# Weight loads issued ahead of the wait for h and p in the gated recurrence of a single-core kernel

## The chip, the cores and the metric

The kernel runs on one core of a Trainium2 chip. The time is the device time of one execution in microseconds; the median of three runs is compared. TensorE (PE) works on a pair of instructions: a weight load (PEld in the profile) puts a 128x128 matrix into the array, and a product (MATMUL) streams the moving operand through it. VectorE (DVE), ScalarE (ACT), GpSimd (POOL) and SyncE (SP, which issues transfers) have queues of their own; semaphores order them.

## The reference, cut to what matters

A mixture of experts (up, gelu, down, four experts and a shared one) is added to x, then a gated recurrence over 1024 time steps runs over the result, for a batch of 2 and 256 features:

```python
def step(h, xs):
    xzt, xrt, xht = xs
    z = jax.nn.sigmoid(xzt + h @ U_z + vz)
    r = jax.nn.sigmoid(xrt + h @ U_r + vr)
    hh = jnp.tanh(xht + r * h @ U + vh)
    h_new = (1.0 - z) * h + z * hh
    return (h_new, h_new)
_, out_t = jax.lax.scan(step, h0, xs)
x = x + jnp.swapaxes(out_t, 0, 1)
```

## The kernel before

The time steps are cut into 16 chunks of 64. Before the loop stands a start of some 55 us (transposes of x, the experts' work on the first chunk, the split of the recurrent matrices). Then a loop over 1024 steps runs the recurrence, and the experts' work on the next chunk is dealt out in small pieces, `side(c, t, window)`, into the two pauses that TensorE has in each step; the order of TensorE's work is written out by hand in that loop.

The recurrent matrices are held as two halves of 16 bits, `u_high` and `u_mid`, and h and p (r times h) likewise as a high and a low part. So each gate takes 12 products a step in `recur`: 8 of the high part (2 output halves x 2 input halves x 2 matrix halves, `HIGH_PRODUCTS`) and 4 of the low part (`LOW_PRODUCTS`). Each product has a weight load of its own, 128x128. One step on TensorE is:

- wait for h_high, 8 products for r; wait for h_low, 4 products for r; the last one signals ScalarE (`preact`);
- 12 products for z, with no wait;
- side work of window 0 (one piece: an `up` or a `down` product of the experts, fp32, which runs as two passes);
- wait for p_high, 8 products for c (the candidate); wait for p_low, 4 products for c; signal;
- side work of window 1 (two pieces). Then the next step.

ScalarE makes tanh of r, z and c as they come (`gate_tanh`, line 395), and one gelu of the side work in some steps (line 389). VectorE makes p_cur from tanh of r and h (line 610), p_low (line 613), the two blend coefficients (lines 618 and 620), then the new h with a scan instruction (line 626), h_low (line 629), half of h (line 630) and the step's output (line 635). The semaphore `part_ready` counts p_high, p_low, h_high and h_low, four a step; TensorE waits on it four times a step. In the last chunk there is no further expert work, and `idle` products of 256 or 384 columns (line 649) stand in the two pauses.

A wait written as `pe.wait_ge` is carried by the instruction that follows it on TensorE. A matrix product written as `mm` becomes a load and a product, and the load, which comes first, carries the wait.

Of the kernel before, what the change touches and what calls it, by code (L numbers as in the profile page):

```python
# [15 lines left out]
P = 128  # L16
GATES = 3
R, Z, C = range(GATES)
# [19 lines left out]
def moe_gru_kernel(nc, x, cond, gate_w, gate_b, time_w, time_b, ew1, eb1, ew2, eb2, sw1, sb1, sw2, sb2,  # L38
                   w_z, u_z, c_z, b_z, w_r, u_r, c_r, b_r, w_h, u_h, c_h, b_h, branch_mask, out):
    B, T, D = x.shape  # L40
    E, _, H = ew1.shape
    BR = E + 1
    KC = D // P
# [81 lines left out]
    with ctx:  # L125
# [3 lines left out]
        def pb(name):  # L129
            return ctx.enter_context(nc.psum_tensor(name, [P, RANK], F32))  # L130
# [67 lines left out]
        gate_ps = [pb("r_ps"), pb("z_ps"), pb("c_ps")]  # L198
# [446 lines left out]
        def _(pe):  # L645
            mm = pe.matmul

            def idle(columns, bank=0, start=False):
                mm(up_ps[bank][:, IDLE_AT:IDLE_AT + columns], ident16[:, :], keep_warm[:, 0:columns],  # L649
                   start=start, stop=True, skip_group_check=True)  # L650
# [3 lines left out]
            for i in range(XT):  # L654
# [4 lines left out]
                for k in range(KC):  # L659
                    for b in range(B):  # L660
                        at = (k * B + b) * P
# [29 lines left out]
            def up(c, i, k):  # L691
                e, j = TILES[c][i]
                n = TILE0[c] + i
                if k == 0:
                    if c <= 1 and j == 0:
                        pe.wait_ge(up_in[e], 16)
                    if n >= 2:
                        pe.wait_ge(gelu_done, n - 1)
                last = mm(up_ps[n % 2][:, 0:COLS], up_w[:, e, k, j * P:(j + 1) * P],  # L699
                          feat[:, k, c * COLS:(c + 1) * COLS], start=(k == 0), stop=(k == KC - 1),  # L700
                          skip_group_check=True)
                if k == KC - 1:
                    last.then_inc(up_done, 1)

            def down(c, i, m):
                e, j = TILES[c][i]
                n = TILE0[c] + i
                if m == 0:
                    if c <= 1 and j == 0:
                        pe.wait_ge(down_in[e], 16)  # L710
                    if e == E:
                        pe.wait_ge(gelu_done, n + 1)
                    elif c == 0:
                        pe.wait_ge(scaled_first, SCALED[n])
                    else:
                        pe.wait_ge(scaled, SCALED[n])
                last = mm(y_ps[:, m * COLS:(m + 1) * COLS], down_w[:, e, j, m * P:(m + 1) * P],  # L717
                          hidden[:, n % TILES_HELD, :], start=False, stop=(m == KC - 1), skip_group_check=True)
                if m == KC - 1:
                    last.then_inc(down_done, 1)  # L720

            def output_bias(c, m):
                if m == 0:
                    if c > 0:
                        pe.wait_ge(feat_ready, c * KC)
                    if c <= 1:
                        pe.wait_ge(rows_made, c + 1)
                mm(y_ps[:, m * COLS:(m + 1) * COLS], bias2_rows[:, m * P:(m + 1) * P],  # L728
                   branch_rows[:, c * COLS:(c + 1) * COLS], start=(m == 0), stop=False, skip_group_check=True)

            def project(c, g, m, k):
                at = (c % 2) * REGION + m * COLS
                mm(gate_ps[g][:, at:at + COLS], wx[:, g, k, m * P:(m + 1) * P], feat[:, k, c * COLS:(c + 1) * COLS],  # L733
                   start=False, stop=False, skip_group_check=True)

            def turn_body(n):
                pe.wait_ge(body_added, n + 1)
                for k in range(KC):
                    last = pe.transpose(rows_ps[:, k * P:(k + 1) * P], out_feat[:, n % 2, k, :], ident[:, :])  # L739
                last.then_inc(turned, 1)  # L740

            first_tiles = len(TILES[0])
            for i in range(first_tiles + FIRST_LAG):
# [4 lines left out]
                if i == 4:  # L748
                    pe.wait_ge(agg_made, 1)
                    for q in range(3):  # L750
                        for k in range(KC):
                            mm(y_ps[0:B, 64 + 2 * E:64 + 3 * E], agg[:, q, k, :], gate_w_sb[:, q, k, :], start=False,
                               stop=False, skip_group_check=True)
                    mm(y_ps[0:B, 64 + 2 * E:64 + 3 * E], ones[0:1, 0:B], bias_row[:, 2 * E:3 * E], start=False,
                       stop=True, skip_group_check=True).then_inc(logits_made, 1)
# [36 lines left out]
            HIGH_PRODUCTS = [(m, k, w) for m in range(KC) for k in range(KC) for w in (u_high, u_mid)]  # L792
            LOW_PRODUCTS = [(m, k, u_high) for m in range(KC) for k in range(KC)]

            def recur(s, g, low, product, last_of_sum=False):
                m, k, w = product
                c, t = divmod(s, CT)
                at = (c % 2) * REGION + m * COLS + t * B

                width = B if last_of_sum else min(FILL if g == C else H_FILL, RANK - at)  # L800
                if g == C:
                    moving = p_low[:, k, 0:width] if low else p_bits[:, k, 1:2 * width:2]
                elif low:
                    moving = h_low[:, 0:width // B, k * B:(k + 1) * B]
                else:
                    moving = h_bits[:, 0:width // B, 4 * k * B + 3:4 * (k + 1) * B:4]
                return mm(gate_ps[g][:, at:at + width], w[:, g, k, m * P:(m + 1) * P], moving, start=False,  # L807
                          stop=last_of_sum, skip_group_check=True)

            def side(c, t, window):  # L810
                for what, *of in SIDE[t, window]:
                    if what == TURN:
                        n = c * BODIES + t // STEPS
                        if n > 0:

                            pe.wait_ge(blended, (c * CT + t + 1) * BLEND_STEP + 2)
                            if n > 1:
                                pe.wait_ge(turned_copied, n - 1)
                            turn_body(n - 1)
                    elif what == IDLE:  # L820
                        if c < CH - 1:

                            idle(IDLE_FILL[window], (TILE0[c + 1] + of[0]) % 2)
                    elif c < CH - 1:
                        i, k = of[0], of[1]
                        if what == UP:
                            up(c + 1, i, k)
                        elif what == DOWN:
                            down(c + 1, i, k)
                        elif what == BIAS:  # L830
                            output_bias(c + 1, k)
                        else:
                            g, m, k = of
                            if m == 0 and k == 0:
                                pe.wait_ge(feat_ready, (c + 2) * KC)
                                pe.wait_ge(seeded, (c + 2) * GATES * KC)
                            if g == Z and k == 0:

                                pe.wait_ge(act_done, (c * CT + t) * GATES + Z + 1)
                            project(c + 1, g, m, k)  # L840

                real = 0 if c == CH - 1 else sum(what != TURN for what, *_ in SIDE[t, window])
                turning = (t, window) in TURNS
                if real == 0 or c == CH - 1:
                    for _ in range(1 + window - turning):
                        idle(IDLE_FILL[window])

            for s in range(T):
                c, t = divmod(s, CT)
                parts = s * PARTS_STEP  # L850
                pe.wait_ge(part_ready, parts + H_HIGH)
                for product in HIGH_PRODUCTS:
                    recur(s, R, False, product)
                pe.wait_ge(part_ready, parts + H_LOW)
                for product in LOW_PRODUCTS:
                    last = recur(s, R, True, product, product is LOW_PRODUCTS[-1])
                last.then_inc(preact, 1)
                for product in HIGH_PRODUCTS:
                    recur(s, Z, False, product)
                for product in LOW_PRODUCTS:  # L860
                    last = recur(s, Z, True, product, product is LOW_PRODUCTS[-1])
                last.then_inc(preact, 1)
                side(c, t, 0)
                pe.wait_ge(part_ready, parts + PARTS_STEP + P_HIGH)
                for product in HIGH_PRODUCTS:
                    recur(s, C, False, product)
                pe.wait_ge(part_ready, parts + PARTS_STEP + P_LOW)
                for product in LOW_PRODUCTS:
                    last = recur(s, C, True, product, product is LOW_PRODUCTS[-1])
                last.then_inc(preact, 1)  # L870
                side(c, t, 1)
# [30 lines left out]
```

## Time and profile before

| what | value |
|---|---|
| median of 3 runs | 1927.91 us (1927.65 to 1928.04) |
| span of the profiled execution, first to last instruction | 1926.4 us |
| own time of the profiled execution | given by its span alone |
| mean granted TensorE clock | 0.994 |
| TensorE products and loads | 42,994 each |
| busy: PE, DVE, ACT | 99%, 62%, 36% |

The span and the median of the runs are 1.5 us apart. The profile is one execution; times are in us from the span's start, starts in a timeline are given to a hundredth. A product's end is modelled, so products that follow each other closely overlap in the records, and the busy share of PE is no measure of how full it is; the starts, and the length of a group of products, can be read. "x4" in a timeline row means that four alike followed each other and are shown as one piece. A window row gives the busy time, overlaps counted once, and the number of instructions in it.

### The profile page before, as it was taken

To read this page: it belongs to the slowest core of one execution; us is meant where nothing else is said; L and a number is where in the kernel's file an instruction comes from. 1 tells how busy PE (TensorE), PEld (TensorE's weight loads), DVE (VectorE), ACT (ScalarE), POOL (GpSimd) and SP (SyncE) were. 2 spreads that over 40 slices of the span, in tenths; PEclk is the share of its full clock that TensorE was granted. 3 is DMA by queue.
4 is the path that set the end of the run, shared out by engine and by line. 5 is a ranking of instruction groups with operands and counts; after the bars stand their busy time and mean duration, and the time that the engine had idled before them with its cause. 6 is when DMAs were issued, how large, how long until landed. Compare 5 with 4: busy or idle time off the path is not lost.

```text
span 1926.4 us, 102805 instructions
## 1 busy us (share of the span) xinstructions
PE 1901.0 (99%) x42994; PEld 1727.7 (90%) x42994; DVE 1190.5 (62%) x8422; ACT 693.7 (36%) x3785; POOL 199.5 (10%) x515
## 2 busy tenths in 40 slices
PE   8999999999999999999999999999999999999998
PEld 8998989989899898999989899898999989999765
DVE  5566656666566665666666566665666656666555
ACT  4333333333333333333333333333333333333222
POOL 0110101101020110101101011010101101011000
PEclk9999999999999999999999999999999999999999
DMA  8000000000000000000000000000000000000000
GB/s 313 3 4 5 5 4 5 5 4 5 4 5 5 4 5 5 4 5 5 4 5 5 4 5 5 4 5 5 4 5 4 5 5 4 5 5 4 5 5 4
DMA packets 16910, 23.69 MB, mean 12 GB/s; under 512 B 3584, under 2 KB 15159, under 8 KB 16444
## 3 DMA queue, kind: packets, MB, share of 16 engines
q1 hardware_dynamic: 15280, 17.05, 2.6%
q8 instruction: 336, 5.51, 1.2%
q14 instruction: 130, 1.06, 0.2%
q10 hardware_dynamic: 1164, 0.07, 0.0%
HBM read 15.01 MB, written 2.10 MB: 9 GB/s over the span
## 4 chain that ended last, share of the span: by engine, by line
PE 96%; DVE 1%; ACT 1%; issue 1%; DMA 0%; SPq 0%; DVEq 0%
PE r_ps L807 20%; PE up_ps L699 19%; PE y_ps L717 19%; PE z_ps L807 16%; PE c_ps L807 16%; DVE h_cur L626 1%; PE up_ps L649 1%; ACT rc_tanh_ps L395 1%; PE c_ps L733 1%; PE z_tanh_ps L739 1%; PE r_ps L733 1%; PE z_ps L733 1%; PE y_ps L728 1%; DMA x_rows<-in_x 0%; PE rc_tanh_ps L662 0%
## 5 line engine op out<-in xcount | busy, mean ns | idle before, releaser
L699 PE MATMUL up_ps<-feat,up_w 128*128 128x128 f32 x2528 | 521.7, 303 | 0.0
L717 PE MATMUL y_ps<-hidden,down_w 128*128 128x128 f32 x2528 | 513.9, 300 | 0.0
L626 DVE TENSOR_TENSOR_SCAN h_cur<-rc_tanh_ps,blend 128x8 f32<-128x8 f32 x1024 | 178.1, 174 | 370.7 <-ACT rc_tanh_ps L395 369.1
L807 PEld LDWEIGHTS r_ps<-h_cur,u_high 128*128 128x128 f16 x4096 | 246.5, 96 | 155.6 <-DVE h_cur L626 74.0
L395 ACT ACTIVATE rc_tanh_ps<-r_ps 128x4 f32<-128x4 f32 x1024 | 161.8, 158 | 594.6 <-PE r_ps L807 594.5
L699 PEld LDWEIGHTS up_ps<-feat,up_w 128*128 128x128 f32 x2528 | 365.5, 191 | 1.1 <-ACT hidden L389 0.6
L807 PE MATMUL r_ps<-h_cur,u_high 128*128 128x20 bf16 (+5 forms) x4096 | 352.0, 180 | 14.4 <-DVE h_cur L626 0.7
L717 PEld LDWEIGHTS y_ps<-hidden,down_w 128*128 128x128 f32 x2528 | 361.6, 190 | 0.4
L807 PE MATMUL c_ps<-p_cur,u_high 128*128 128x40 bf16 (+10 forms) x4096 | 342.0, 180 | 1.8
L807 PE MATMUL c_ps<-p_cur,u_mid 128*128 128x40 bf16 (+10 forms) x4096 | 337.5, 179 | 0.0
L807 PE MATMUL r_ps<-h_cur,u_mid 128*128 128x20 bf16 (+5 forms) x4096 | 337.2, 178 | 0.0
L807 PE MATMUL z_ps<-h_cur,u_high 128*128 128x20 bf16 (+5 forms) x4096 | 337.1, 178 | 0.0
L807 PE MATMUL z_ps<-h_cur,u_mid 128*128 128x20 bf16 (+5 forms) x4096 | 336.6, 178 | 0.0
L610 DVE SCALAR_TENSOR_TENSOR p_cur<-rc_tanh_ps,h_cur 128x4 f32<-128x4 f32 x1024 | 166.7, 163 | 262.6 <-ACT rc_tanh_ps L395 257.9
L395 ACT ACTIVATE rc_tanh_ps<-c_ps 128x4 f32<-128x4 f32 x1024 | 161.8, 158 | 463.2 <-PE c_ps L807 463.2
L280 POOL TENSOR_TENSOR hidden<-hidden,expert_w 128x128 f32<-128x128 f32 (+3 forms) x416 | 164.1, 394 | 1379.8 <-ACT hidden L389 1379.8
L635 DVE SCALAR_TENSOR_TENSOR out_feat<-h_cur,h_unscale,feat 128x4 f32<-128x4 f32 x1024 | 296.0, 289 | 0.0
L807 PEld LDWEIGHTS c_ps<-p_cur,u_high 128*128 128x128 f16 x4096 | 255.9, 96 | 28.4 <-DVE p_cur L610 22.7
L807 PEld LDWEIGHTS r_ps<-h_cur,u_mid 128*128 128x128 f16 x4096 | 257.4, 97 | 0.0
L807 PEld LDWEIGHTS c_ps<-p_cur,u_mid 128*128 128x128 f16 x4096 | 256.7, 97 | 0.4
L807 PEld LDWEIGHTS z_ps<-h_cur,u_mid 128*128 128x128 f16 x4096 | 251.8, 96 | 0.0
L807 PEld LDWEIGHTS z_ps<-h_cur,u_high 128*128 128x128 f16 x4096 | 251.2, 95 | 0.0
(141 smaller groups left out, 2952.5 us busy)
## 6 DMA issues: line engine op xcount, KB each, us to landing
up_w<-in_L_cond_ew SPq DMA_DIRECT2D x4, 1024.0 KB, 9.7
down_w<-in_L_cond_ew SPq DMA_DIRECT2D x4, 1024.0 KB, 10.3
x_rows<-in_x SPq DMA_DIRECT2D x8, 256.0 KB, 4.3
out<-out_rows SPq DMA_DIRECT2D x128, 16.0 KB, 1.8
up_w<-in_L_cond_sw SPq DMA_DIRECT2D x1, 1024.0 KB, 12.7
down_w<-in_L_cond_sw SPq DMA_DIRECT2D x1, 1024.0 KB, 13.5
cf<-in_L_cond_C_r SPq DMA_DIRECT2D x1, 256.0 KB, 9.5
cf<-in_L_cond_C_z SPq DMA_DIRECT2D x1, 256.0 KB, 9.6
```

The costliest lines, as they stand in the source:

```text
L280: ins = engine.tensor_tensor(cols, cols, w, ALU.mult)
L395: act.activation((tanh_r, tanh_z, c_now)[g].rearrange("p (m b) -> p m b", b=B), gate_v[g][:, c % 2, :, t, :], ACT.Tanh, scale=0.5 / GAIN). ...
L610: dve.scalar_tensor_tensor(p_cur[:, :, 0:B], sq(tanh_r), 1.0, sq(h_now), ALU.add, ALU.mult).then_inc(part_ready, 1)
L626: dve.tensor_tensor_scan(h_cur[:, 0, :], cand, blend[:, :], 0.0, ALU.mult, ALU.add).then_inc(part_ready, 1)
L635: last = dve.scalar_tensor_tensor(out_feat[:, body % 2, :, row * B:(row + 1) * B], sq(h_now), h_unscale[:, :], feat[:, :, s * B:(s + 1) * ...
L649: mm(up_ps[bank][:, IDLE_AT:IDLE_AT + columns], ident16[:, :], keep_warm[:, 0:columns], start=start, stop=True, skip_group_check=True)
L699: last = mm(up_ps[n % 2][:, 0:COLS], up_w[:, e, k, j * P:(j + 1) * P], feat[:, k, c * COLS:(c + 1) * COLS], start=(k == 0), stop=(k == KC ...
L717: last = mm(y_ps[:, m * COLS:(m + 1) * COLS], down_w[:, e, j, m * P:(m + 1) * P], hidden[:, n % TILES_HELD, :], start=False, stop=(m == KC ...
L728: mm(y_ps[:, m * COLS:(m + 1) * COLS], bias2_rows[:, m * P:(m + 1) * P], branch_rows[:, c * COLS:(c + 1) * COLS], start=(m == 0), stop=Fal ...
L733: mm(gate_ps[g][:, at:at + COLS], wx[:, g, k, m * P:(m + 1) * P], feat[:, k, c * COLS:(c + 1) * COLS], start=False, stop=False, skip_group ...
L739: last = pe.transpose(rows_ps[:, k * P:(k + 1) * P], out_feat[:, n % 2, k, :], ident[:, :])
L807: return mm(gate_ps[g][:, at:at + width], w[:, g, k, m * P:(m + 1) * P], moving, start=False, stop=last_of_sum, skip_group_check=True)
```

## The change

In the loop, the first load of each of the four waiting groups of a step is written out by itself and placed ahead of the wait; the first product of the group is then written as an instruction that finds its weights loaded, and it alone carries the wait. The other products, the z group and the side work stay as they are. All four loads are of `u_high`.

```diff
+            def load(g, product):
+                m, k, w = product
+                pe.ldweights(w[:, g, k, m * P:(m + 1) * P])
+
+            def multiply_loaded(to, weights, moving, stop):
+                return pe.add_instruction(mybir.InstMatmult(
+                    name=nc.get_next_instruction_name(), engine=mybir.EngineType.PE,
+                    ins=[pe.lower_ap(moving), pe.lower_ap(weights, for_matmul_weights=True)],
+                    outs=[pe.lower_ap(to)], start_tensor_calc=False, stop_tensor_calc=stop, ldweights=False,
+                    tile_size=(P, P), tile_position=(0, 0), bass_skip_group_check=True))
+
-            def recur(s, g, low, product, last_of_sum=False):
+            def recur(s, g, low, product, last_of_sum=False, loaded=False):
...
+                if loaded:
+                    return multiply_loaded(gate_ps[g][:, at:at + width], w[:, g, k, m * P:(m + 1) * P], moving,
+                                           last_of_sum)
...
+                load(R, HIGH_PRODUCTS[0])
                 pe.wait_ge(part_ready, parts + H_HIGH)
-                for product in HIGH_PRODUCTS:
+                recur(s, R, False, HIGH_PRODUCTS[0], loaded=True)
+                for product in HIGH_PRODUCTS[1:]:
                     recur(s, R, False, product)
+                load(R, LOW_PRODUCTS[0])
                 pe.wait_ge(part_ready, parts + H_LOW)
-                for product in LOW_PRODUCTS:
+                recur(s, R, True, LOW_PRODUCTS[0], loaded=True)
+                for product in LOW_PRODUCTS[1:]:
                     last = recur(s, R, True, product, product is LOW_PRODUCTS[-1])
...
+                load(C, HIGH_PRODUCTS[0])
                 pe.wait_ge(part_ready, parts + PARTS_STEP + P_HIGH)
-                for product in HIGH_PRODUCTS:
+                recur(s, C, False, HIGH_PRODUCTS[0], loaded=True)
+                for product in HIGH_PRODUCTS[1:]:
                     recur(s, C, False, product)
+                load(C, LOW_PRODUCTS[0])
                 pe.wait_ge(part_ready, parts + PARTS_STEP + P_LOW)
-                for product in LOW_PRODUCTS:
+                recur(s, C, True, LOW_PRODUCTS[0], loaded=True)
+                for product in LOW_PRODUCTS[1:]:
                     last = recur(s, C, True, product, product is LOW_PRODUCTS[-1])
```

The start of r on TensorE, with the last pieces of side work ahead of it, in the kernel before. In these rows a MATMUL of line 807 (821 in the changed kernel) is a load and a product together; one of line 800 is a product alone.

```order
L807 MATMUL c_ps<-p_low,u_high 128x2
L699 MATMUL up_ps<-feat,up_w 128x128
L717 MATMUL y_ps<-hidden,down_w 128x128 [waits scaled]
L807 MATMUL r_ps<-h_cur,u_high 128x20 [waits part_ready]
L807 MATMUL r_ps<-h_cur,u_mid 128x20
```

The same place in the changed kernel:

```order
L821 MATMUL c_ps<-p_low,u_high 128x2
L699 MATMUL up_ps<-feat,up_w 128x128
L717 MATMUL y_ps<-hidden,down_w 128x128 [waits scaled]
L797 LDWEIGHTS u_high
L800 MATMUL r_ps<-h_cur,u_high 128x20 [waits part_ready]
L821 MATMUL r_ps<-h_cur,u_mid 128x20
```

The load stands behind the side product and ahead of the wait; nothing that waits lies between.

The passage from the high to the low products of r on TensorE, before:

```order
L807 MATMUL r_ps<-h_cur,u_high 128x20
L807 MATMUL r_ps<-h_cur,u_mid 128x20
L807 MATMUL r_ps<-h_low,u_high 128x20 [waits part_ready]
L807 MATMUL r_ps<-h_low,u_high 128x20 x2
L807 MATMUL r_ps<-h_low,u_high 128x2
```

and in the changed kernel:

```order
L821 MATMUL r_ps<-h_cur,u_high 128x20
L821 MATMUL r_ps<-h_cur,u_mid 128x20
L797 LDWEIGHTS u_high
L800 MATMUL r_ps<-h_low,u_high 128x20 [waits part_ready]
L821 MATMUL r_ps<-h_low,u_high 128x20 x2
L821 MATMUL r_ps<-h_low,u_high 128x2
```

Here the load follows the eighth high product directly, and the first low product waits for h_low alone.

The start of c on TensorE, behind the z group and one piece of side work, in the changed kernel (before, the rows of lines 797 and 800 are one row of line 807 with the wait):

```order
L821 MATMUL z_ps<-h_low,u_high 128x20 x3
L821 MATMUL z_ps<-h_low,u_high 128x2
L699 MATMUL up_ps<-feat,up_w 128x128 [waits gelu_done]
L797 LDWEIGHTS u_high
L800 MATMUL c_ps<-p_cur,u_high 128x40 [waits part_ready]
L821 MATMUL c_ps<-p_cur,u_mid 128x40
```

The side product and its own wait for a gelu stay ahead of the load.

## Rows read from the trace of the kernel before

**Rows 1.** The page, part 1: busy time, share, instructions of each engine.

```profile
PE 1901.0 (99%) x42994; PEld 1727.7 (90%) x42994; DVE 1190.5 (62%) x8422; ACT 693.7 (36%) x3785; POOL 199.5 (10%) x515
```

**Rows 2.** The page, part 4: the chain that ended last, by engine.

```profile
PE 96%; DVE 1%; ACT 1%; issue 1%; DMA 0%; SPq 0%; DVEq 0%
```

**Rows 3.** Waits: who waited for whom, us in total, times, longest.

```profile
ACT rc_tanh_ps L395 <- PE r_ps L807: 594.5, 1023, 8.6
ACT rc_tanh_ps L395 <- PE c_ps L807: 463.2, 1024, 0.9
DVE h_cur L626 <- ACT rc_tanh_ps L395: 369.1, 1008, 0.8
```

**Rows 4.** Timeline at the start of r: start, us, engine, line, operation, tiles.

```profile
1002.08 0.17 DVE L626 TENSOR_TENSOR_SCAN h_cur<-rc_tanh_ps,blend 128x8 f32<-128x8 f32 x1 [0.38 <-ACT rc_tanh_ps L395]
1002.29 0.16 DVE L629 TENSOR_TENSOR h_low<-h_cur 128x4 f16<-128x4 f32 x1
1002.30 0.10 PEld L807 LDWEIGHTS r_ps<-h_cur,u_high 128*128 128x128 f16 x1
1002.31 0.18 PE L807 MATMUL r_ps<-h_cur,u_high 128*128 128x20 bf16 x1
1002.32 0.10 PEld L807 LDWEIGHTS r_ps<-h_cur,u_mid 128*128 128x128 f16 x1
1002.35 0.18 PE L807 MATMUL r_ps<-h_cur,u_mid 128*128 128x20 bf16 x1
...
1002.50 0.18 PE L807 MATMUL r_ps<-h_cur,u_mid 128*128 128x20 bf16 x1
1002.50 0.17 PEld L807 LDWEIGHTS r_ps<-h_low,u_high 128*128 128x128 f16 x4
1002.52 0.24 PE L807 MATMUL r_ps<-h_low,u_high 128*128 128x20 f16 x4
```

**Rows 5.** r products in two windows: stretch, its us, PE busy (instructions), clock, DMA.

```profile
1004.11:1077.03 72.92, 18.09 (x480) 1.00 0.02 5
1820.72:1878.83 58.11, 14.47 (x384) 1.00 0.02 5
```

**Rows 6.** z products in the same two windows.

```profile
1004.11:1077.03 72.92, 17.52 (x480) 1.00 0.02 5
1820.72:1878.83 58.11, 14.02 (x384) 1.00 0.02 5
```

**Rows 7.** c products in the same two windows.

```profile
1004.11:1077.03 72.92, 17.72 (x480) 1.00 0.02 5
1820.72:1878.83 58.11, 14.49 (x384) 1.00 0.02 5
```

**Rows 8.** Timeline around the start of c, and the side work of a second window.

```profile
1001.71 0.47 PE L717 MATMUL y_ps<-hidden,down_w 128*128 128x128 f32 x2
...
1002.02 0.39 PE L699 MATMUL up_ps<-feat,up_w 128*128 128x128 f32 x2
...
1002.92 0.47 PE L699 MATMUL up_ps<-feat,up_w 128*128 128x128 f32 x2
1002.99 0.16 DVE L610 SCALAR_TENSOR_TENSOR p_cur<-rc_tanh_ps,h_cur 128x4 f32<-128x4 f32 x1 [0.17 <-ACT rc_tanh_ps L395]
...
1003.21 0.10 PEld L807 LDWEIGHTS c_ps<-p_cur,u_high 128*128 128x128 f16 x1
1003.23 0.18 PE L807 MATMUL c_ps<-p_cur,u_high 128*128 128x40 bf16 x1
```

**Rows 9.** Timeline at the start of c in the last 64 steps.

```profile
1821.42 0.16 DVE L610 SCALAR_TENSOR_TENSOR p_cur<-rc_tanh_ps,h_cur 128x4 f32<-128x4 f32 x1 [0.34 <-ACT rc_tanh_ps L395]
...
1821.64 0.10 PEld L807 LDWEIGHTS c_ps<-p_cur,u_high 128*128 128x128 f16 x1 [0.21 <-DVE p_cur L610]
1821.64 0.19 PE L807 MATMUL c_ps<-p_cur,u_high 128*128 128x40 bf16 x1
```

## The prediction

> **What bounds the kernel now.** I read the page's busy shares first, then its chain, then the waits, then the timeline of single steps. The first two are a trap: TensorE is 99% busy and 96% of the chain [rows 1, 2]. But the end of a product is modelled, not seen, and side work has been laid into every pause. The waits tell more: ScalarE waits about a thousand times each for the r products and for the c products, and VectorE as often for ScalarE [rows 3]. So the loop is a ring: c products, tanh, scan, r products, tanh, p, c products. It goes round in 72.92 us for 40 steps (480 r products, 12 a step), 1.823 us each [rows 5], and what shortens that ring shortens 1024 steps.
>
> In the ring the reader should look at two joints of TensorE.
>
> The r joint [rows 4]: the scan ends at 1002.08 + 0.17 = 1002.25. The first r load starts at 1002.30, its product at 1002.31, the second load at 1002.32, the second product only at 1002.35. From there the eighth is reached at 1002.50: 0.15 us for 6 products, 25 ns each. So the first spacing is 40 ns where the others are 25. The same is seen without rounding in the length of a whole group of 12 products, from the start of the first to the end of the last: r takes 18.09 us / 40 = 452.3 ns [rows 5]; z, which follows with no wait and has each load ahead, takes 17.52 / 40 = 438.0 ns [rows 6]. Thus **14 ns a step** are lost at the start of r.
>
> The c joint [rows 8]: a side product in two passes starts at 1002.92, the first c load at 1003.21, its product at 1003.23, 0.31 us after the side product. In the other window of a step a side product is followed by another one after the same 0.31 us (1001.71 to 1002.02). So the first c product starts when the array is free of the side work, and the load, 0.02 us earlier, is already hidden. The c group takes 17.72 / 40 = 443.0 ns [rows 7], 5 ns over z. In the last 64 steps, where short idle products stand in place of side work, c has the r pattern: load and product in the same hundredth [rows 9], and 14.49 / 32 = 452.8 ns a group [rows 7].
>
> **The change, part by part.** Nothing is added or removed: a row of r products in the old order is a load and a product by itself (42,994 of each in [rows 1]), and compiled, the new program has as many of both with the same operands. Four waits a step go from a load to the product behind it. No DMA, and no queue but TensorE's, is touched; the z group and the side work stay behind the same waits as before.
>
> *First r load.* It can now run in the pause before r: the next instruction on TensorE after the last side product, with nothing before it that waits. The pause covers it wholly. If that cover were gone, the load would stand where it stands now and cost what it costs now. What is saved: (a) the product may start where the load starts now, 0 to 10 ns earlier by the rows; I take 4. (b) the second product may follow at less than 40 ns. No product of the trace carries a wait, so (b) is bounded by rows. Upper end: the z group, 452.3 - 438.0 = 14 ns. Lower end: 0, if the slow spacing belongs to the restart and not to the load. Nearest row: the c group with side work, whose load is in about 0.02 us before its product can go: 452.3 - 443.0 = 9 ns. Together (a) and (b): 4 to 18 ns, and I take 4 + 9 = **13 ns**.
>
> *First low r load.* This one decides whether the 13 ns are kept. h_low ends at 1002.29 + 0.16 = 1002.45, its load starts at 1002.50, its product at 1002.52 [rows 4]. The eighth high product starts at 1002.50, and 25 ns later would be 1002.52 or 1002.53 too. The low load therefore sits right at its wait, as the other loads after a release do, 0.05 us behind VectorE. If the high products move up by 13 ns and the low load stayed behind the wait, the low product could not move at all. With the load ahead, the product may go from about 1002.50, so 20 ns can pass, and 13 go through with 7 to spare. The hoisted load itself follows the eighth product as all loads do, at no cost.
>
> *z, side work, tanh, p.* They follow r with fixed distances, so they move up by the same 13 ns; VectorE and ScalarE have pauses in each step ([rows 3]).
>
> *First c load.* With side work: the array stays the limit, and only the 5 ns over z are to be had. I take 2, between 0 and 5. In the last 64 steps there is no such limit: 13 as for r, 4 to 18.
>
> *First low c load.* It stands in the rhythm of the products already and p_low is early: 0.
>
> Sum: 1024 x 13 = 13.3 us for r, 960 x 2 = 1.9 for c, 64 x 13 = 0.8 for c at the end: 16.1 us. The profiled execution has a span of 1926.4 us and the median of the runs is 1927.91, 1.5 us around it that the change doesn't touch. 1926.4 - 16.1 = 1910.3, and with the 1.5 us **1911.8 us**, 0.8% faster.
>
> **What speaks against.** In the rows the first r product starts 0.01 us behind its load, while in the rhythm a product follows its load by more (1002.32 to 1002.35) [rows 4]. A product thus seems to be able to start before its load is through. The Trainium skill ("TensorE: Matmul & The Clock Gate", section on the array as 16 32×32 arrays) says just this: MATMUL can begin before LDWEIGHTS completes. Taken by itself it would leave part (a) alone, 4 ns a joint, which is the small gain priced below; the trace agrees for the start of the first product, but the 40 ns to the second speak for the load still being paid.
>
> **Rivals.**
> *Small gain.* The 40 ns belong to TensorE coming out of a wait (the second load can't be issued sooner behind the instruction that waited), so (b) is 0. For: the pattern is the same at every released start, r or late c [rows 4, 9]. Against: c with side work comes out of its wait 0.02 us before the array is free and loses only 5 ns. Price: 4 x 1024 + 4 x 64 = 4.4 us saved, 1923.6 us.
>
> *The wait goes to the low products.* r starts earlier, but the low product, now waiting by itself, still starts 0.07 us behind h_low as today, because a product needs as long after its release as load and product now do together. r gains nothing; c keeps 1.9 + 0.8: 1925.2 us. For: h_low is the next thing late, by 0.02 us. Against: at the r joint load and product together need only 0.06 us from the scan's end to the product.
>
> *Slower.* A product that carries a wait may start later after its release than a load does, because its operand is read only then; no row shows one. If it starts 0.02 us later than a load would (1003.21 to 1003.23 is the distance from a load to its product at the c joint; unrounded I take 23 ns), then r's first product is 23 - 4 = 19 ns later, its second follows at 28 instead of 40 ns, and r loses 7 ns; c loses 1 with side work and 7 without. It decides from about 16 ns of such a delay, where what the second product wins is used up. Price: 7 x 1024 + 960 + 7 x 64 = 8.6 us more, 1936.5 us. Against: VectorE and ScalarE carry their waits on the very instructions that compute, and VectorE starts h_low 0.04 us after the scan's end, less than the 0.05 of TensorE's load.
>
> *The change doesn't do what it says.* If the load were held behind the wait all the same, or the order didn't change, the time would be today's. The order of the built program excludes the second; the first I count with the case of no gain.
>
> **How the numbers follow.** Forecast, r gaining 9 to 18 ns: 0.61 (with 0.03 for its upper edge). Small gain: 0.15. Wait goes to the low products or no gain: 0.11. Slower: 0.13. The measurement can tell about 0.2%, 3.9 us, from no change. The forecast lies wholly beyond it; the small gain lies at its edge, and I give 0.09 of its 0.15 to faster: 0.70. Same: 0.06 + 0.11 = 0.17. Slower: 0.13. The lower end of the range is every bound at its best: 1024 x 18 + 960 x 5 + 64 x 18 = 24.4 us, 1903.5. The upper end takes in the small gain and the low-product case, 1926. Left out is the slower case, 0.13, and a little at the bottom.
>
> **What would show it.** In the changed trace the first r load should start right behind the last side product and not 0.05 us behind the scan; the r group should last about 443 ns instead of 452 in the same stretch; the step 1.808 us instead of 1.823; the low r product should start 0.05 to 0.06 us after h_low. The c group should stay near 443 ns with side work. If r's second product still comes 40 ns behind the first, it is the small gain; if r's first spacing is 25 to 30 ns but the low product starts 0.07 us behind h_low, the wait has moved on; if the first r product starts 0.08 us after the scan's end, the slower case. I am wrong altogether if the steps change in a part that holds none of these four loads.

## The result, and the profile after

The changed kernel takes **1903.9 us** (median of 4 runs, 1902.25 to 1914.42) against 1927.8 us before (median of 4): the ratio is 0.989, with a 95% interval of 0.9874 to 0.9905. The forecast was 1911.8 us with a range of 1903.5 to 1926.0. The direction and the place were right; the gain is 24 us where 16 were forecast, at the upper edge of what the bounds allowed.

The busy shares of the changed kernel, part 1 of its page, say as little as in [rows 1]; one product's record is missing from the trace:

```profile
PE 1876.4 (99%) x42993; PEld 1728.7 (91%) x42994; DVE 1191.2 (63%) x8422; ACT 693.7 (37%) x3785; POOL 199.6 (11%) x515
```

The waits of the changed kernel, the rows that answer to [rows 3] (who waited for whom: us in total, times, longest):

```profile
ACT rc_tanh_ps L395 <- PE r_ps L821: 574.7, 1023, 8.6
ACT rc_tanh_ps L395 <- PE c_ps L821: 457.7, 1024, 0.5
DVE h_cur L626 <- ACT rc_tanh_ps L395: 363.0, 1008, 0.5
```

ScalarE waits 20 us less for r (594.5 before), 5 to 6 us less for c. The start of r in the changed kernel's timeline, which answers to [rows 4] (start, us, engine, line, operation, tiles):

```profile
1000.91 0.17 DVE L626 TENSOR_TENSOR_SCAN h_cur<-rc_tanh_ps,blend 128x8 f32<-128x8 f32 x1 [0.38 <-ACT rc_tanh_ps L395]
1000.97 0.10 PEld L797 LDWEIGHTS <-u_high 128*128 128x128 f16 x1
1001.12 0.17 DVE L629 TENSOR_TENSOR h_low<-h_cur 128x4 f16<-128x4 f32 x1
1001.14 0.18 PE L800 MATMUL r_ps<-h_cur,u_high 128*128 128x20 bf16 x1
1001.14 0.10 PEld L821 LDWEIGHTS r_ps<-h_cur,u_mid 128*128 128x128 f16 x1
1001.16 0.18 PE L821 MATMUL r_ps<-h_cur,u_mid 128*128 128x20 bf16 x1
...
1001.32 0.18 PE L821 MATMUL r_ps<-h_cur,u_mid 128*128 128x20 bf16 x1
1001.32 0.10 PEld L797 LDWEIGHTS <-u_high 128*128 128x128 f16 x1
1001.34 0.17 PE L800 MATMUL r_ps<-h_low,u_high 128*128 128x20 f16 x1
```

The load (line 797) starts 0.17 us ahead of its product, while VectorE still scans; unrounded it stands 2 ns behind the start of the last pass of side work, as the prediction's first sign asks. The product starts 0.06 us after the scan's end (1001.08) by these rounded rows; the load of before started 0.05 us after it, and unrounded both are 53 ns. The second product follows at once in the rhythm of the others: the eighth starts 0.18 us after the first, where it was 0.19. The low load sits in that rhythm too, and the low product starts 0.05 us after h_low's end (1001.29), no longer 0.07.

The lengths of the groups, in windows of 40 and of 32 steps (stretch, its us, PE busy with count, clock, DMA). First r, which answers to [rows 5]:

```profile
990.24:1062.37 72.13, 17.55 (x480) 1.00 0.02 5
1796.51:1853.50 56.99, 14.03 (x384) 1.00 0.02 5
```

then c, which answers to [rows 7]:

```profile
990.24:1062.37 72.13, 17.68 (x480) 1.00 0.02 5
1796.51:1853.50 56.99, 14.05 (x384) 1.00 0.02 5
```

An r group, from the start of its first product to the end of its last, now takes 17.55 / 40 = 438.8 ns (452.3 before), as short as z with 438.0 [rows 6]. A c group with side work takes 442.0 (443.0), in the last 64 steps 14.05 / 32 = 439.1 (452.8). The 40 steps take 72.13 us where they took 72.92: 20 ns a step; the 32 of the last chunk 56.99 where they took 58.11: 35 ns a step.

Read to the nanosecond in the starts of the trace, the medians over all steps are:

| stretch | before | changed |
|---|---|---|
| scan's end to first r product | 57 ns | 53 ns |
| first to second r product | 39 | 25 |
| h_low's end to first low r product | 74 | 55 |
| p_cur's end to first c product, with side work | 75 | 76 |
| the same, last 64 steps | 57 | 53 |
| first to second c product, last 64 steps | 39 | 25 |
| step, with side work | 1820 | 1800 |
| step, last 64 | 1811 | 1774 |

In a later execution of the changed kernel the last 64 steps take 1778 ns each, so 33 to 37 ns are saved there. One released load cost **18 ns**: 4 to its product and 14 more to the second.

### The profile page after: what moved, and what is told of

The parts are those of the page before. It is cut to its first block, busy times and chain, and to the rows that moved or that the text cites. A ratio compares the mean times of both kernels' runs of the same rounds, so it can differ in the third digit from the quotient of the medians.

```text
span 1900.5 us, 102803 instructions
## 1 busy us (share of the span) xinstructions
PE 1876.4 (99%) x42993; PEld 1728.7 (91%) x42994; DVE 1191.2 (63%) x8422; ACT 693.7 (37%) x3785; POOL 199.6 (11%) x515
## 4 chain that ended last, share of the span: by engine, by line
PE 96%; DVE 1%; ACT 1%; issue 1%; DMA 0%; SPq 0%; DVEq 0%
PE up_ps L699 19%; PE y_ps L717 19%; PE z_ps L821 16%; PE r_ps L821 13%; PE c_ps L821 13%; PE r_ps L800 6%; PE c_ps L800 3%; DVE h_cur L626 1%; PE up_ps L649 1%; ACT rc_tanh_ps L395 1%; PE c_ps L733 1%; PE z_tanh_ps L739 1%; PE r_ps L733 1%; PE z_ps L733 1%; PE y_ps L728 1%
## 5 line engine op out<-in xcount | busy, mean ns | idle before, releaser
L797 PEld LDWEIGHTS <-u_high 128*128 128x128 f16 x4096 | 399.3, 97 | 8.2
L821 PEld LDWEIGHTS r_ps<-h_cur,u_mid 128*128 128x128 f16 x4096 | 252.3, 96 | 118.1 <-issue 51.9
L821 PE MATMUL c_ps<-p_cur,u_high 128*128 128x40 bf16 (+6 forms) x3072 | 285.4, 179 | 0.0
L821 PE MATMUL r_ps<-h_cur,u_high 128*128 128x20 bf16 (+3 forms) x3072 | 285.3, 178 | 0.0
L821 PE MATMUL z_ps<-h_low,u_high 128*128 128x20 f16 (+1 forms) x4096 | 243.7, 169 | 0.0
```

What stands on the lines that cost most here:

```text
L797: pe.ldweights(w[:, g, k, m * P:(m + 1) * P])
```

## The experiments

All were run on the chip beside the kernel before, whose median was 1926 to 1928 us. Theory: a load behind a wait costs 18 ns in the ring; at r both loads have to move; at c with side work little or nothing is to be had. "The joint" is the place where TensorE takes up work again after a wait; "the rhythm" is the even distance of products that follow each other without one.

### r alone

```diff
-                load(C, HIGH_PRODUCTS[0])          (c as in the kernel before, high and low)
```

> Both r loads (high and low) ahead of their waits, the c loads as before. Theory (the r joint gives 18 ns a step: the first product 4 ns earlier behind the scan, the second 25 instead of 39 ns behind it): 1024 x 18 = 18.4 us saved, 1909.4 us, step 1802 ns in the chunks with side work. Rival (the joints are not separate, c's load gives the larger part): less than 10 us saved.

Measured: 1905.4 us (1904.6 to 1906.0), ratio 0.9886 (0.987 to 0.9903), 22 us saved where the theory gave 18. The step with side work is 1800 ns where 1802 were expected: the same 20 ns shorter as with all four loads, 2 more than the joint's 18. The rival falls: nearly everything comes from r.

### Only the high r load

```diff
                 load(R, HIGH_PRODUCTS[0])
                 pe.wait_ge(part_ready, parts + H_HIGH)
...
-                load(R, LOW_PRODUCTS[0])
                 pe.wait_ge(part_ready, parts + H_LOW)
-                recur(s, R, True, LOW_PRODUCTS[0], loaded=True)
+                (all low products with their loads behind the wait; c as before)
```

> Only the load of the first high r product is ahead; the low one stays behind the wait for h_low. Theory (the low load starts 52 ns behind h_low whatever the high products do, and its product 21 ns later): the last r product doesn't move, 0 to 2 us saved, 1926 to 1928 us, with the eighth high product 18 ns earlier than before and a hole of that size ahead of the low product. Rival (the low products simply follow the high ones): as with both, 1909 us.

Measured: 1924.2 us (10 runs, 1921.5 to 1926.8), ratio 0.9982 (0.9972 to 0.9991). Of the 18 ns the step keeps 3 (1817 ns). The time lies below the theory's 1926 to 1928 us, the rival's 1909 is far off, and the theory was wrong on how the rest is lost. Its timeline at the passage to the low products:

```profile
1001.29 0.16 DVE L629 TENSOR_TENSOR h_low<-h_cur 128x4 f16<-128x4 f32 x1
1001.31 0.18 PE L800 MATMUL r_ps<-h_cur,u_high 128*128 128x20 bf16 x1
...
1001.48 0.18 PE L821 MATMUL r_ps<-h_cur,u_mid 128*128 128x20 bf16 x1
1001.51 0.16 PEld L821 LDWEIGHTS r_ps<-h_low,u_high 128*128 128x128 f16 x4
1001.51 0.25 PE L821 MATMUL r_ps<-h_low,u_high 128*128 128x20 f16 x4
```

The low load starts with its product at 1001.51, 0.06 us behind h_low. There is no hole ahead of that product (26 ns behind the eighth); the price comes behind it, at 38 ns to the second low product: the pattern of a released load has wandered from the high to the low products.

### Only the low r load

```diff
-                load(R, HIGH_PRODUCTS[0])          (high products as before, c as before)
...
                 load(R, LOW_PRODUCTS[0])
                 pe.wait_ge(part_ready, parts + H_LOW)
```

> Only the load of the first low r product is ahead; the high one stays behind its wait. Theory (the low product already follows the eighth high one after 25 ns, the rhythm of all products): nothing saved, 1926 to 1928 us. Rival (h_low is the later of the two, so the low load alone is what counts): up to 18 ns a step, 1909 us.

Measured: 1928.7 us, ratio 1.0004 (0.9995 to 1.0014); step 1820 ns. As the theory said, nothing. Neither r load is worth anything much by itself (3 and 0 ns); together they are worth 20.

### c alone

```diff
-                load(R, HIGH_PRODUCTS[0])          (r as in the kernel before, high and low)
```

> Both c loads ahead, the r loads as before. Theory (with side work the array is busy until the first c product; 2 ns a step there, 18 in the last 64 steps): 960 x 2 + 64 x 18 = 3.1 us saved, 1924.8 us. Rival (c gains like r): 1024 x 18, 1909 us.

Measured: 1924.3 us, ratio 0.9986 (0.9977 to 0.9996). Steps with side work stay at 1820 ns; the last 64 fall from 1811 to 1794. So the c loads bring 64 x 17 = 1.1 us and not the 2 ns a step elsewhere; of the 3.3 us measured the rest is within the interval, which reaches from 0.8 to 4.4 us. The rival (c gains like r) falls.

### One load more behind the wait

```diff
                 pe.wait_ge(part_ready, parts + H_HIGH)
+                load(R, HIGH_PRODUCTS[0])
                 for product in HIGH_PRODUCTS:
```

> The kernel before, with one load more behind the wait for h_high: the first r load is issued twice in a row there, so that the cost of one load behind the wait is measured by itself. Theory (a load behind the wait is paid in the ring): 14 to 25 ns more a step, 1024 of them, 14 to 26 us slower, 1942 to 1954 us. Rival (a load behind a wait runs beside the start of its product and the slow first spacing belongs to the restart): within 4 us of 1927.9.

Measured: 1970.4 us, ratio 1.0219 (1.0206 to 1.0232): 42 us slower, 40 ns a step. The rival falls, but the theory's size too (14 to 26 us). The start of r in its timeline:

```profile
1000.93 0.10 PEld L797 LDWEIGHTS <-u_high 128*128 128x128 f16 x1
1000.97 0.10 PEld L821 LDWEIGHTS r_ps<-h_cur,u_high 128*128 128x128 f16 x1
1000.98 0.18 PE L821 MATMUL r_ps<-h_cur,u_high 128*128 128x20 bf16 x1
1000.99 0.10 PEld L821 LDWEIGHTS r_ps<-h_cur,u_mid 128*128 128x128 f16 x1
1001.01 0.18 PE L821 MATMUL r_ps<-h_cur,u_mid 128*128 128x20 bf16 x1
```

The second load starts 40 ns behind the first, and then the whole pattern of a released load follows once more: 4 ns to its product, 11 more to the next load, 28 more to the next product. Removing a load gives 18 and adding one takes 40: was it the empty pipeline, or two loads in a row?

### Two loads in a row in the middle of z

```diff
                 for product in HIGH_PRODUCTS:
+                    if product is HIGH_PRODUCTS[4]:
+                        load(Z, product)
                     recur(s, Z, False, product)
```

> The changed kernel with one load issued twice in a row in the middle of the z group, where nothing waits. Theory A (two loads with no product between them cost 40 ns anywhere, because the second finds no free place for its weights until the first is through): 15 to 40 ns more a step, 15 to 41 us slower, 1919 to 1946 us. Theory B (the 40 ns that a second load cost behind the wait belong to the empty pipeline): within 5 us of 1904.

Measured: 1933.7 us, ratio 1.0041 (1.0026 to 1.0055) to the kernel before; against the changed kernel's 1903.9, on which it stands, about 30 us slower. Theory A holds in its cost; its reason, that the second load finds no free place, is not shown. The z loads in its timeline:

```profile
1001.03 0.10 PEld L821 LDWEIGHTS z_ps<-h_cur,u_mid 128*128 128x128 f16 x1
1001.06 0.10 PEld L797 LDWEIGHTS <-u_high 128*128 128x128 f16 x1
1001.10 0.10 PEld L821 LDWEIGHTS z_ps<-h_cur,u_high 128*128 128x128 f16 x1
1001.11 0.10 PEld L821 LDWEIGHTS z_ps<-h_cur,u_mid 128*128 128x128 f16 x1
1001.14 0.10 PEld L821 LDWEIGHTS z_ps<-h_cur,u_high 128*128 128x128 f16 x1
```

Nothing waits there, TensorE is in full rhythm, and again the second of two loads in a row comes 0.04 us behind the first, with the slow pattern behind it. So the pattern needs no wait on a semaphore. What its cases share is a load that comes late: it starts 4 ns ahead of its product, where in the rhythm a load starts 23 ns ahead. That holds behind a release, behind another load, and in the run with only the high r load, where products are still running. Why the product behind a late load comes 14 ns late was not tried. The steps with side work are 33 ns longer (1833); the last 64 take 1778 ns, as in the second execution of the changed kernel: in place of side work stand short idle products there, and the longer z doesn't reach c, which still starts 54 ns behind p_cur.

### Two loads ahead of the wait

```diff
                 load(R, HIGH_PRODUCTS[0])
+                load(R, HIGH_PRODUCTS[0])
                 pe.wait_ge(part_ready, parts + H_HIGH)
```

> The changed kernel with the first r load issued twice in a row ahead of the wait. Theory (a load costs only what of it lies behind the release; the pause ahead of r is 66 ns and more): no change, 1902 to 1906 us. Rival (the second load delays r wherever it stands): 15 ns a step and more, 1919 us and above.

Measured: 1903.4 us (1903.0 to 1903.5), step 1800 ns: free, as the theory says. The pause ahead of r covers two loads as well as one; in its trace they start 121 and 76 ns before the scan's end.

### z on 8 loads

```diff
-                for product in HIGH_PRODUCTS:
-                    recur(s, Z, False, product)
+                for m, k, w in HIGH_PRODUCTS:
+                    if w is u_mid:
+                        recur(s, Z, False, (m, k, w))
                 for product in LOW_PRODUCTS:
-                    last = recur(s, Z, True, product, product is LOW_PRODUCTS[-1])
+                    recur(s, Z, False, product)
+                    last = recur(s, Z, True, product, product is LOW_PRODUCTS[-1], loaded=True)
```

> The changed kernel, with the z group's 12 products on 8 loads: the high and the low product on the same u_high share one load (the sum is made in another order). If the 25 ns between products are the load's (a load waits for the product ahead to start, a product for its load), z gets shorter by 4 x 10 to 17 ns, the side work of window 0 ends earlier, and c is no longer held by the array: 20 to 23 ns a step in 960 steps, 1904 - 20 = 1882 to 1884 us. If 25 ns is the least distance of two products whatever is loaded: z keeps 275 ns from its first to its last product, 1903 to 1904 us.

Measured: 1903.9 us (1903.0 to 1904.9), step 1800 ns: the same as the changed kernel. The z products in its timeline; those of line 800 have no load of their own:

```profile
1000.31 0.18 PE L821 MATMUL z_ps<-h_cur,u_high 128*128 128x20 bf16 x1
1000.34 0.17 PE L800 MATMUL z_ps<-h_low,u_high 128*128 128x20 f16 x1
1000.36 0.18 PE L821 MATMUL z_ps<-h_cur,u_high 128*128 128x20 bf16 x1
1000.39 0.17 PE L800 MATMUL z_ps<-h_low,u_high 128*128 128x20 f16 x1
```

They stand 25 ns apart with a load or without. So 25 ns is the distance of products here, and loads in the rhythm are free. The Trainium skill ("TensorE: Matmul & The Clock Gate", section "Wait — 56ns, not 53.3ns?") says that start-to-start never drops below about 25 ns however small the moving operand; this trace agrees, for 20 columns and without a load between.

### The changed kernel again, and its spread

No edit.

> The changed kernel once more, for the spread. At full clock in the loop a step is 20 ns shorter in 960 steps and 37 ns in 64: 21.6 us less than before. Theory: the first result's difference of 23.9 us holds some 2 us of stretches at half the clock, which the profile of before has (three in the loop) and that of the changed kernel has not; so executions without such a stretch come to about 1902 us and each stretch adds 1.5 to 3.5 us. Rival: the whole difference is the loads', and every execution without disturbance lies within 0.5 us of another.

Measured: 1905.2 us, six runs, each with its mean granted clock: 1901.96 (0.998), 1902.84 (0.998), 1903.79 (0.996), 1906.62 (0.991), 1911.33 (0.988), 1915.08 (0.984). The rival falls: the lower the clock, the longer the time. The windows of the kernel before around 520 us (stretch, us, then busy time and count of PE, PEld, DVE, ACT, POOL, then clock, DMA):

```profile
505.00:519.00 14.00, 13.72 (x323) 11.82 (x319) 8.29 (x63) 3.79 (x24) 0.00 (x0) 1.00 0.01 3
519.00:530.00 11.00, 10.76 (x206) 9.28 (x206) 5.81 (x42) 3.58 (x19) 0.80 (x2) 0.69 0.02 5
```

and one window of this run of the changed kernel:

```profile
1210.00:1217.00 7.00, 6.89 (x123) 6.33 (x122) 3.31 (x25) 1.81 (x11) 0.40 (x1) 0.51 0.02 4
```

At about 521 us of the kernel before the clock goes to the lower level, 1.2 GHz, for 6.8 us, right after a chunk's last steps, which have idle products in place of side work. Ahead of the last chunk, the profile of before has three such stretches in the loop (6.8, 3.4 and 3.4 us), that of the changed kernel none, and this run five of 6.8 us: its loop, from first to last scan, takes 1849.0 us where the one without takes 1840.2, so 1.8 us for each. The expectation for executions without such a stretch, about 1902 us, is met: the first profile of the changed kernel, which has none, is of an execution of 1902.25 us.

The place is the same everywhere. The eleven profiles of kernels that deal out side work and idle products as here (before, changed, and all experiments but the next three) have 18 such stretches ahead of the last chunk: 17 begin in the first step of a chunk, one in step 58 of one.

### More idle products

```diff
-IDLE_FILL = (256, 384)
+IDLE_FILL = (384, 384)
...
-                    for _ in range(1 + window - turning):
+                    for _ in range(1 + 2 * window - turning):
```

> The changed kernel with more idle products in the windows without side work: 384 columns in place of 256 in window 0, and three in place of two in window 1. Theory (the spread of the changed kernel, 1902 to 1915 us, comes from stretches at half clock that begin after the chunk's thin last steps): hardly any such stretch in the loop, 1901 to 1903 us, all executions within 2 us. Rival (the stretches come from elsewhere): the spread stays, 1902 to 1915 us; or the longer idle products reach into the r and c joints and cost time in the last 64 steps.

Measured: 1902.3 us, four runs from 1901.6 to 1902.8. The profile has no stretch at half clock in the loop; the spread is 1.3 us where it was 13. One of the four is recorded with a mean clock of 0.948 at 1901.6 us, which doesn't go with its time and stays open. The expectation is met, but four runs don't show that the edit is the cause: two loads ahead of the wait, with the idle products as they were, gave four runs within 0.5 us, and three of the eleven profiles above have no stretch either. That the stretches begin at a chunk's end is shown by their places; that longer idle products prevent them is not.

### Side work dealt out otherwise

```diff
+SPARED = (9, 18, 27, 36, 45)
...
-            while units and len(SIDE[t, w]) < 1 + w:
+            while units and len(SIDE[t, w]) < (1 + w if w or t not in SPARED else 0):
...
-                if real == 0 or c == CH - 1:
+                if (real == 0 and (window or t not in SPARED)) or c == CH - 1:
```

> The changed kernel with the empty places of side work dealt out otherwise: window 0 is left empty in steps 9, 18, 27, 36 and 45 of a chunk, so that side work fills the chunk's last steps further (7 empty windows 0 a chunk in place of 3, and 2 wholly empty windows 1 in place of 4). Theory (c waits for the array behind the side work of window 0, about 25 ns a step; the clock is halved after the idle steps at a chunk's end): 4 x 25 ns x 15 chunks = 1.5 us saved at full clock, and fewer stretches at half clock than the 0 to 5 seen: 1900 to 1902 us, against 1904 to 1905. Rival (c is held by something else, and where the empty windows lie doesn't matter): 1904 to 1905 us.

Measured: 1901.2 us (1899.3 to 1901.6), ratio 0.9864 (0.9849 to 0.9878). Its loop takes 1839.1 us where the changed kernel's without a clock stretch takes 1840.2: 1.1 us of the 1.5 expected. The scans around a step 18 (line 627 in this kernel) in its timeline:

```profile
1006.09 0.17 DVE L627 TENSOR_TENSOR_SCAN h_cur<-rc_tanh_ps,blend 128x8 f32<-128x8 f32 x1 [0.38 <-ACT rc_tanh_ps L396]
1007.88 0.17 DVE L627 TENSOR_TENSOR_SCAN h_cur<-rc_tanh_ps,blend 128x8 f32<-128x8 f32 x1 [0.38 <-ACT rc_tanh_ps L396]
1009.66 0.17 DVE L627 TENSOR_TENSOR_SCAN h_cur<-rc_tanh_ps,blend 128x8 f32<-128x8 f32 x1 [0.35 <-ACT rc_tanh_ps L396]
1011.46 0.17 DVE L627 TENSOR_TENSOR_SCAN h_cur<-rc_tanh_ps,blend 128x8 f32<-128x8 f32 x1 [0.38 <-ACT rc_tanh_ps L396]
```

The spared step, which ends with the scan at 1009.66, takes 1.78 us; by the medians over all chunks, the spared steps take 1778 ns and their neighbours 1800. So 22 ns, not 25, are had where c has no side work ahead of it, and the rival falls. Its profile has no stretch at half clock in the loop; as above, one profile and four runs don't show that the edit is the reason.

### Both of these

```diff
+SPARED = (9, 18, 27, 36, 45)
+IDLE_FILL = (384, 384)                             (and three idle products in window 1)
...                                                 (the other lines as in the two edits above)
```

> Both of the last two edits on the changed kernel: side work dealt out as with five spared windows 0, and the longer idle products. Theory (the two take away different things: 4 empty windows more a chunk are worth 25 ns each, 1.5 us, and the idle products keep the clock up at the chunk's end): 1899 to 1901 us, all executions within 2 us. Rival (with the side work spread out the clock already holds, and longer idle products add nothing): 1900 to 1902 us, like the spread alone.

Measured: 1901.1 us (1900.8 to 1901.5), ratio 0.9867 (0.9851 to 0.9884). The median is that of the dealt-out side work alone, as the rival says, and its loop takes 1838.9 us against 1839.1; all four runs lie within 0.7 us of another. By their medians these last two are the fastest versions, some 3 us below the changed kernel; against its executions at about 1902 us only the 1 us of the shorter steps is left, and the intervals of the three ratios overlap.

## Why the prediction was right or wrong

**Where the time goes: right at r, incomplete for the ring.** The r joint and its slow first spacing carried the gain; r alone gives 22 of the 24 us. But the ring as it was written, from r over tanh and p to c, is not the path in steps with side work. There c waits for TensorE's own queue: z, the side product, c. Its first product comes 76 ns behind p_cur where 53 suffice in the last 64 steps, 33 ns more in z make the step 33 longer, and a step with an empty window 0 is 22 ns shorter. The prediction's c joint says as much, and since that queue starts with r, the sum for r stands.

**The first r load: right in mechanism, too small.** Part (a) was taken as 4 ns and is 4. Part (b) was taken as 9 ns, from the c group with side work as the nearest row, and is 14, the upper bound from the z group. The mis-sized term is the choice of the nearest row: a c group is 4 to 5 ns over z for a reason of its own, which it keeps in the changed kernel (442.0 ns against 438.0) with its load ahead of the wait. About 3 ns of it are c's first spacing, 28 ns behind a side product in both kernels, where it is 25 in the last 64 steps of the changed one; why it is longer there was not tried. With 18 in place of 13 the sum is 1024 x 18 = 18.4 us for r.

**The first low r load: right.** It decides: without it 15 of the 18 ns are lost, with it the low product starts 55 ns after h_low. The margin that was left at 7 ns has shrunk to about 2: with 18 ns passed, the rhythm and the release come nearly together (25 ns behind the eighth product, 55 behind h_low, where r and the late c start 53 after their release). How it is lost without the low load was told wrongly: the low product can move, but its successor pays.

**The first c load: too much with side work, too little without.** 2 ns were taken for 960 steps and the c loads alone gave 0 there; 13 were taken for the last 64 and 17 came. The array, held by the side product, is the limit, as said. The step with side work is 20 ns shorter all the same, and all 20 come with the r loads. The 2 beyond the joint's 18 lie behind c's first product: from the first to the last start of c it is 278 to 279 ns where it was 280, and tanh follows 200 ns later where it was 201. Why, stays open; single nanoseconds also differ between executions.

**The sum.** 960 x 20 + 64 x 37 = 21.6 us in the loop at full clock, which alone would give 1906.2 us. The sum had no term for the clock. The two profiles show its part: the loop, from first to last scan, takes 1865.6 us before and 1840.2 after, 25.4 less, and the 13.6 us at half clock that only the loop of before has ahead of the last chunk are worth 3.6 of that at 1.8 us for 6.8. In the medians 2.3 of the 24 us are left for it, a little more than one stretch of 6.8 us; which executions had how many isn't recorded. So that the time came so near the lower end of the range, 1903.5 us, is in part luck.

**The rivals.** The small gain fell: the slow spacing is the load's, since it goes with the load and comes back where a second load stands directly behind another. The sentence of the Trainium skill behind it ("TensorE: Matmul & The Clock Gate", section "Architectural detail: the array is 16× 32×32, not 1× 128×128"), that MATMUL can begin before LDWEIGHTS completes, is true of the records: the product starts 4 ns after a load whose record lasts 0.10 us. But what is saved at the first product is paid at the second, 39 ns behind it in place of 25. The wait that goes to the low products fell too: the low product, waiting by itself, starts 55 ns behind h_low and not 74. When the low load is left behind, the gain is lost there all the same, but by the second low product, 38 ns behind the first. The slower case fell: a product that carries its wait starts 53 ns after the scan's end, exactly as late as a load did.

## What to carry to other kernels

Where TensorE waits on the path for a fresh moving operand and the weights are known long before, put the load ahead of the wait, into the pause. Do it at every wait that follows closely, since one that is left behind takes the gain back (3 of 18 ns stayed). Inside the rhythm a load was free (z on 8 loads); a second one directly behind it was not, unless a pause covered both. Before counting on a joint, look whether the array or the release is the later of the two there.

## What the runs showed of the hardware that was not expected

- Two weight loads in a row, with no product between, start 39 to 40 ns apart, behind a wait and in full rhythm alike, and the next products come 4 and 43 ns after the second load, not 25 apart. One such load cost 40 ns a step at r and 33 in z; in the pause ahead of r, where the two start 45 ns apart, it cost nothing.
- A product that finds its weights loaded starts 53 ns after VectorE's scan ends, as a load did, and the next one follows after 25 ns.
- Twelve products on eight loads take as long as twelve on twelve: 25 ns each.
- In some executions the granted clock falls to half for 3.4 or 6.8 us, 17 of 18 times in the first step behind a chunk's last steps with idle products; 6.8 us of it cost 1.8 us in the loop. With longer idle products or spread side work none was seen in three profiles, which is too few to call it a remedy.
